# PSUM evacuations of the projection phase: from ScalarE to VectorE

## The reference

```python
def _L0_attn_ref(x, Wq, Wk, Wv, Wo):
    q = x @ Wq
    k = x @ Wk
    v = x @ Wv
    scores = einsum('bsd,btd->bst', q, k)      # causal mask
    attn = softmax(scores * dim_k ** (-0.5))
    return einsum('bst,btv->bsv', attn, v) @ Wo

x = x + _layernorm(_L0_attn_ref(_layernorm(x), Wq, Wk, Wv, Wo))
x = x + _layernorm(_L0_ffn_ref(_layernorm(x), ...))
```

## Time and profile before

| | |
|---|---|
| timed runs | 5034.3 and 5038.12 us, median 5036.21 |
| profiled execution | 5067.08 us |
| its span, slowest core (core 4) | 5065.5 us; the cores from 5017.9 to 5065.5 |
| busy share of the span | TensorE 54%, ScalarE 30%, VectorE 23%, POOL 4% |
| transposes (L185) | first 15.4, last 336.9 us; their copies L189 x256, 68.3 us busy |
| K groups (L231) | 348.6 to 461.2 us; casts L238 x64, 37.5 us, 586 ns each |
| V groups (L255) | 484.5 to 605.3 us; casts L262 x64, 37.5 us |
| Q groups (L286) | 630.3 to 824.9 us; casts L293 x64, 37.5 us |
| idle of TensorE ahead of the three stages, until the last weight cast L213 | K 11.4, V 22.9, Q 24.6 us |

### The profile page before, as it was taken

One profiled execution on the slowest core, in us unless ns is written; L12 is line 12 of the kernel. 1 busy time (PEld: TensorE's weight loads), 2 busy tenths in 40 slices (PEclk: granted clock), 3 DMA queues, 4 the chain that ended last, 5 costly groups with the idle time before them and its releaser, 6 DMA issues.

```text
span 5065.5 us, 39323 instructions; the slowest of 8 cores (5017.9 to 5065.5 us)
## 1 busy us (share of the span) xinstructions
PE 2737.8 (54%) x12112; PEld 1136.7 (22%) x12112; DVE 1159.1 (23%) x2336; ACT 1518.2 (30%) x2849; POOL 218.2 (4%) x404
## 2 busy tenths in 40 slices
PE   1238764455566667742222656656465565556564
PEld 0013321122233333321100222212122122222121
DVE  1110000322221211122211232223222322223222
ACT  4432211222222222222211333334333433333333
POOL 0000111000111111100000000000000000000000
PEclk9999997667778778865555777768677777768676
DMA  2121212222233233322210001010101001010100
GB/s 56 54 58 42 92 43 86 71 88 85 86 94 98 84 98 100 98 73 71 75 40 21 21 22 33 13 54 13 50 17 46 21 9 46 13 54 13 46 21 29
DMA packets 129702, 270.18 MB, mean 53 GB/s; under 512 B 29718, under 2 KB 70934, under 8 KB 129500
## 3 DMA queue, kind: packets, MB, share of 16 engines
q1 hardware_dynamic: 74460, 137.62, 9.3%
q0 software_dynamic: 32000, 104.88, 6.7%
q10 hardware_dynamic: 23040, 25.18, 1.4%
HBM read 208.89 MB, written 58.72 MB: 53 GB/s over the span
## 4 chain that ended last, share of the span: by engine, by line
PE 41%; ACT 19%; DVE 15%; issue 14%; DMA 9%; SPq 1%; DVEq 1%; ACTq 1%; POOLq 0%; POOL 0%
PE PB L848 7%; PE PB L430 5%; PE PB L391 5%; DVE stp L119 3%; PE PB L778 3%; ACT L134 3%; ACT sqd L121 3%; DVE zbuf L798 2%; ACT gT L825 2%; PE PB L231 2%; PE PB L820 2%; PE PB L642 2%; ACT wT L648 2%; PE PB L493 2%; PE PB L832 2%
## 5 line engine op out<-in xcount | busy, mean ns | idle before, releaser
L778 PE MATMUL PB<-wT,hTb 128*128 128x512 bf16 x1536 | 446.4, 443 | 147.2 <-DVE zbuf L804 127.1
L848 PE MATMUL PB<-gT,wT 128*128 128x512 bf16 x1536 | 387.9, 398 | 22.1 <-ACT raT L837 22.1
L121 ACT ACTIVATE sqd<-PB 128x1024 bf16<-128x1024 f32 x160 | 162.5, 1016 | 717.5 <-DVE stp L119 555.2
L820 PE MATMUL PB<-ident,g_sb 128*128 128x128 bf16 x768 | 118.4, 294 | 461.0 <-ACT g_sb L811 322.3
L391 PE MATMUL PB<-qbuf,kT 128*128 128x256 bf16 x2176 | 306.3, 289 | 34.0 <-DMA qbuf<-qTs 34.0
L865 DVE TENSOR_TENSOR hTf<-PB,hTf 128x512 f32<-128x512 f32 x192 | 132.8, 692 | 800.0 <-PE PB L860 800.0
L430 PE MATMUL PB<-vbuf,expT 128*128 128x512 bf16 x1088 | 286.0, 386 | 0.8 <-DMA vbuf<-vs 0.8
L119 DVE TENSOR_REDUCE stp<-PB 128x1 f32<-128x1024 f32 x160 | 195.1, 1220 | 369.7 <-PE PB L791 256.3
L391 PEld LDWEIGHTS PB<-qbuf,kT 128*128 128x128 bf16 x2176 | 224.1, 103 | 122.5 <-issue 35.0
L778 PEld LDWEIGHTS PB<-wT,hTb 128*128 128x128 bf16 x1536 | 150.6, 107 | 427.8 <-issue 325.2
L642 PE MATMUL PB<-ident,dqb 128*128 128x128 bf16 x384 | 101.3, 264 | 268.4 <-ACT wT L648 168.9
(11 more groups left out here) (100 smaller groups left out, 3453.5 us busy)
## 6 DMA issues: line engine op xcount, KB each, us to landing
vbuf<-vs POOLq DMA_DIRECT2D x272, 256.0 KB, 2.9
qwt<-qw SPq DMA_DIRECT2D x48, 512.0 KB, 3.5
xtile<-x SPq DMA_DIRECT2D x32, 512.0 KB, 4.1
x_res<-x SPq DMA_DIRECT2D x32, 512.0 KB, 5.3
x2s<-x_sb ACTq DMA_DIRECT2D x32, 512.0 KB, 5.4
x2res<-x2s SPq DMA_DIRECT2D x32, 512.0 KB, 3.9
out<-x2res POOLq DMA_DIRECT2D x32, 512.0 KB, 3.0
gmb<-gm SPq DMA_DIRECT2D x24, 512.0 KB, 4.2
```

The source lines that it names most:

```text
L121: t2 = emit("s", lambda e: e.activation(out=sqd[:, 0:W], in_=src_ap, func=AF.Square, accum_out=sq_ap), deps + war + (t1,))
L778: pY=pY: e.matmul(pY[:, oc * 512:(oc + 1) * 512], hTb[:, j * 512 + ssi * 128: j * 512 + (ssi + 1) * 128], wT[:, l1 * NJ * 1024 + j * 1024 ...
L820: ttr = emit("t", lambda e, j=j, ssi=ssi: e.transpose(pTc[:, ssi * 128:(ssi + 1) * 128], g_sb[:, ssi * 1024 + j * 128: ssi * 1024 + (j + 1 ...
L848: tmm = emit("t", lambda e, j=j, oo=oo, l2=l2, zsl=zsl: e.matmul(pZ[:, zsl * 512:(zsl + 1) * 512], wT[:, l2 * NJ * 1024 + j * 1024 + oo * 128:
```

## The change

The four kinds of PSUM evacuation of the projection phase are emitted to VectorE's stream as `tensor_copy`, where they were `copy` on ScalarE's: the copy behind each transpose, and the casts of K, V and Q. Their waits, their operands, the tiles and the order of the source stay. The tokens that they give (`tev`) are now VectorE's, so transposes, matmul groups, weight loads and POOL transfers that waited for ScalarE's evacuation wait for VectorE's.

```diff
--- before.py
+++ after.py
@@ -186,8 +186,8 @@
                             pa, na[:, j * 128:(j + 1) * 128], ident[:]),
                             (tap, t_id, pTa_rd[0]))
                         dst = xnT[:, j * S + tt * 128: j * S + (tt + 1) * 128]
-                        tev = emit("s", lambda e, pa=pa, dst=dst: e.copy(out=dst, in_=pa),
-                                   (ttr,))
+                        tev = emit("v", lambda e, pa=pa, dst=dst: e.tensor_copy(
+                            out=dst, in_=pa), (ttr,))
                         pTa_rd[0] = tev
                         xnT_tok[(j, tt)] = tev
                         last_ev = tev
@@ -235,8 +235,8 @@
                                 start=(j == 0), stop=(j == NJ - 1)),
                                 dep0 if j == 0 else ())
                         dst = kT[:, m * S + tc * 512: m * S + (tc + 1) * 512]
-                        tev = emit("s", lambda e, pa=pa, dst=dst: e.copy(out=dst, in_=pa),
-                                   (tmm,))
+                        tev = emit("v", lambda e, pa=pa, dst=dst: e.tensor_copy(
+                            out=dst, in_=pa), (tmm,))
                         pP_rd[psl] = tev
                         kT_tok[(m, tc)] = tev
                 kT_done[0] = tev
```

## The result

| | before | after |
|---|---|---|
| all timed runs, median | 5068.19 us (13 runs, 5034.3 to 5116.3) | 5095.99 us (14 runs, 5085.9 to 5175.17) |
| ratio | | 1.0097, 95% interval 1.0061 to 1.0132 |
| profiled execution, its span | 5067.08, 5065.5 us | 5126.20, 5124.7 us (core 5) |
| transpose stage | 333.0 us | 377.4 us |
| K, V, Q stages | 112.4, 119.6, 178.7 us | 111.9, 121.8, 181.9 us |

A forecast was written before the change was run, and what follows sets the result against it. Transpose stage: ScalarE, TensorE and VectorE take turns on one chain; K: TensorE bounds; Q and partly V: POOL spills hold TensorE. Terms -6.9+40.3+7.4+0.1+3.4+1.7 = +46 us on 5036 gave 5082 us, range 5060 to 5112.

The forecast's parts named there:

- (a): Transpose stage: a turn of transpose and copy takes 0.74 us, 0.027 less than before; 256 turns give -6.9 us.
- rival C: Transpose stage: the new copy costs as much as the 256-wide one, +17 us, 5099 us in all; chance 7%.
- term b: Transpose stage: the next tile's reduction, behind the moved copies, delays the Square 1.30 us on 31 tiles, +40.3 us.
- (c): End of transpose stage: wk's weight casts stand behind the last tile's copies on VectorE, +7.4 us.
- (d, e): K: only the last cast counts, +0.1 us; V and Q: evacuations 0.106 us longer ahead of spills, +1.7 and +3.4 us.
- Rivals A and B: TensorE's clock: A, in Q, 5127 or 5060 us, 8% each way; B, falling in V, over 2% slower, 4%.
- the sign that I had set: Q stage: the prediction is wrong if Q changes by more than 5 us; that stretch's clock would then tell why.

## Why the prediction was right or wrong, step by step

**Turn of transpose and copy (a): right,** but for a turn counted twice. 225 ns foretold, 224 measured; turn 0.74. The bounds of 159 and 291 ns were not needed, and rival C fell. From a tile's first transpose to its last copy it is 5.73 us in the earlier trace rows and 5.55 after (220.46 to 226.01), 0.18 less and not 8 x 0.027, as the eighth copy's own duration is in term b already: 32 tiles give -5.8 us for the -6.9. The Trainium skill's "VectorE: DVE Perf Modes", section "The TRN2 errata", would have given 192 and 658 ns; the two forms took 224 and 692, about 33 ns more each, as the row of the 256-wide copy had said.

**The uncovered reduction (b): right,** in its mechanism and size. 1.30 us a tile foretold, 1.45-0.16 = 1.29 in the trace, 31 x 1.29 = 40 us; the run with the reduction ahead and the Square held gives 35.5 us, against 31 x 1.13 expected of it.

**The wk casts (c): right.** +7.4 foretold; 7.0 by the median of the cores, each against itself. Undoing a part of it gave 5.8 us.

**K, V, Q (d, e): right,** with small sizes. Casts of 692 ns; K unchanged; V +2.2 in the whole change and +2.9 alone where 1.7 was foretold, Q +3.2 and +2.8 where it was 3.4. The waits for the spills grew with them (3.5 to 6.2 and 55.6 to 59.0 us). In part it was luck that Q came out: the cycle was read on core 4, whose Q of 194.6 us was not repeated. After the change the same core took 181.9, so by the sign that I had set, Q changing by more than 5 us, that core would have spoken against me; the medians of the cores don't.

**A term was missing.** The change turned two waits on one semaphore into waits on two, 0.11 us a tile, 3.4 us in all; the run with the other order gives 3.5 us back. I had put it at nothing by writing "with the same waits". The tokens were the same, the semaphores were not. With it the terms of the transpose stage are -5.8+40+7.0+3.4 = 44.6 us against 44.4 measured, where the prediction had 40.8.

**Rivals A and B fell.** Q took 178.6 to 188.6 us on the cores after, 172.5 to 194.8 before; V 121.4 to 122.6. The section "HAM oscillation" of the Trainium skill's "TensorE: Matmul & The Clock Gate" tells of bursts that start at a low clock behind waits for transfers. The earlier trace rows agree in part: one group behind a wait of 2.24 us ran at the low level, the next behind a wait of 2.20 us at the high one. Waiting 0.1 us more did not make it worse.

**The step that failed is the last one, from the sum to "no change".** The sum of 46 us, 0.91%, stands beside a measured 0.97%. But I wrote that 0.9% "is inside the 2% that a measurement of this kernel can tell from no change", and gave 95% to a time within 2% of before, in which a loss of 1% and no change are one. The runs showed a change that is told apart from none: the interval, 1.0061 to 1.0132, excludes 1, and so does that of the half with the transposes' copies alone, 1.0067 to 1.0106. A forecast that rests on a fixed chain of 31 equal tiles should have been given as what it was: slower by 1%. The profile had the means to say so, since the stage of 333 us differs by 1.5 us between the cores. The absolute figure was weaker than the difference: 5082 us starts from two runs, 5036.2 us. The median of all runs is 5068.2 before and 5096.0 after, so 5082 lies 14 us under the one and only 0.3% over the other, though the change is 1.0%; nothing in the prediction said how far the start itself might move.

## What to carry to other kernels

The price of moving an instruction to another engine is read less from its own duration than from what stands behind it in the new queue, and from what stood behind it in the old one: here copies 43 ns shorter cost 44 us, and the same copies come with a gain of 45 us once the next tile's first step is emitted ahead of them. Where small copies alternate with small transposes, first ask for one wide copy; it was worth 120 us of the stage on the old engine, without any move. And name the wait that is released last as the last one in the list.

## What the runs showed of the hardware that was not expected

A second wait on TensorE, on another semaphore and satisfied over 5 us before, costs 0.11 us when it stands behind the one that is released last (0.25 against 0.14 us from the normalization's end to the transpose), and nothing ahead of it. Eight transposes into one PSUM tile without a wait between them take 1.01 us on TensorE, where eight turns with a copy between them took 5.9 to 6.1 us; and a copy of 1024 bf16 elements from PSUM with a strided output takes 691 ns on VectorE and 1.01 us on ScalarE, both on the straight line through the short ones (159 ns for 2 and 291 for 256 elements on VectorE; 267 ns for 128 and, with an f32 source, 586 for 512 on ScalarE).
